# How q and k travel through DRAM in a multi-level attention kernel: long row runs against equal blocks of 16 rows

## The reference

```python
for lvl in range(4):
    x = query[:, ::2 ** lvl, :]
    q, k, v = split(x @ w_in[lvl].T + b_in[lvl])         # 16 heads of 16
    attn = softmax(q @ k.T / sqrt(16))
    outs.append((attn @ v) @ w_out[lvl].T + b_out[lvl])
current = outs[3]
for lvl in (2, 1, 0):
    current = upsample(current) @ up_w[lvl].T + up_b[lvl] + outs[lvl]
x = layernorm(x + current)
h = silu(x @ w1.T * s1) * (x @ w2.T * s2)
h = gelu(gelu(h @ h1.T * g1) @ h2.T * g2)
y = layernorm(x + h @ w3.T * s3)
```

## Time and profile before

| | us |
|---|---|
| median of 3 runs | 4259.68 |
| lowest and highest run | 4255.66, 4264.0 |
| the profiled execution | 4264.0 |
| its span, first to last instruction | 4262.2 |
| one regular batch of attention, from 1101.23 to 1431.91 us | 330.7 |

### The profile page before, as it was taken

How to read it: one execution, slowest core, us unless ns; L and a number is a source line. 1 busy time by engine, 2 the same in 40 slices (tenths; PEclk the granted TensorE clock), 3 DMA queues, 4 the chain that set the end, 5 groups by cost and what they waited for, 6 DMA issues and landing times. The chain is left out here.

```text
span 4262.2 us, 69758 instructions
## 1 busy us (share of the span) xinstructions
PE 3845.1 (90%) x20881; PEld 2140.1 (50%) x20881; DVE 2564.2 (60%) x4681; ACT 2486.9 (58%) x3261; POOL 1210.9 (28%) x1144
## 2 busy tenths in 40 slices
PE   4599999999989999989999999819999999999998
PEld 2233434434334433433433333207887787877887
DVE  2377787787787787787787788553333333333333
ACT  1377767767767767767767767624444433444343
POOL 4234444444434434534434442210000000000000
PEclk8699999999999999999999999959999999999999
DMA  5434434434333434333433432160000000000000
GB/s 184 107 79 98 102 90 104 101 87 98 100 91 89 109 73 111 101 81 98 108 90 83 115 89 57 34 237 6 13 18 11 11 11 21 11 11 12 17 14 11
DMA packets 277100, 307.45 MB, mean 72 GB/s; under 512 B 68000, under 2 KB 228960, under 8 KB 276448
## 3 DMA queue, kind: packets, MB, share of 16 engines
q1 hardware_dynamic: 267456, 293.56, 27.1%
q10 hardware_dynamic: 9216, 8.39, 0.6%
HBM read 202.28 MB, written 96.47 MB: 70 GB/s over the span
## 5 line engine op out<-in xcount | busy, mean ns | idle before, releaser
L766 ACT ACTIVATE a_probs<-a_p_s 128x1024 f32<-128x1024 f32 x1360 | 1326.4, 1021 | 625.4 <-PE a_p_s L1008 617.5
L847 DVE TENSOR_REDUCE a_part_max<-a_p_m 128x1 f32<-128x512 f32 x2048 | 1335.8, 680 | 407.1 <-PE a_p_m L1023 403.0
L1023 PE MATMUL a_p_m<-a_k_st,a_q_st 96*128 96x512 bf16 (+2 forms) x2944 | 1008.6, 375 | 172.7 <-DVE a_part_max L847 74.1
L1403 PE MATMUL p_h<-f_h_hi,f_w_hi 128*128 128x512 f32 x2048 | 810.2, 396 | 41.0 <-issue 38.7
L1008 PE MATMUL a_p_s<-a_q_st,a_k_st 98*128 98x512 bf16 (+2 forms) x2944 | 823.0, 367 | 3.2 <-DMA a_q_st<-a_neg_bf 2.3
L1403 PE MATMUL p_h<-f_h_lo,f_w_hi 128*128 128x512 f32 x2048 | 807.0, 394 | 1.8 <-issue 1.8
L1023 PEld LDWEIGHTS a_p_m<-a_k_st,a_q_st 96*128 96x128 bf16 x2944 | 257.5, 97 | 1068.2 <-DVE a_part_max L847 681.1
L1040 PE MATMUL a_p_o<-a_probs,a_v_aug 128*17 128x512 f32 (+2 forms) x5888 | 727.4, 573 | 0.8 <-ACT a_probs L766 0.8
L1372 DVE TENSOR_TENSOR f_h_lo<-f_h_f,f_h_hi 128x512 fp32r<-128x512 f32 x256 | 177.3, 693 | 722.4 <-ACT f_h_hi L1285 722.4
L847 DVE TENSOR_REDUCE a_row_max<-a_p_m 128x1 f32<-128x512 f32 (+2 forms) x672 | 439.9, 680 | 183.8 <-PE a_p_m L1023 178.0
L1283 ACT ACTIVATE f_h_f<-p_h,f_sc 128x512 f32<-128x512 f32 x256 | 176.6, 690 | 584.8 <-PE p_h L1403 584.7
(11 more groups left out here) (116 smaller groups left out, 4550.6 us busy)
## 6 DMA issues: line engine op xcount, KB each, us to landing
qk_scratch<-a_qk_bf SPq DMA_DIRECT2D x288, 128.0 KB
a_w_lo<-wqkv_inner SPq DMA_DIRECT2D x32, 768.0 KB, 5.0
a_q_st<-qk_scratch SPq DMA_DIRECT2D x32, 384.0 KB, 5.3
a_k_st<-qk_scratch SPq DMA_DIRECT2D x32, 384.0 KB, 6.8
a_a_lo<-a_attn SPq DMA_DIRECT2D x384, 32.0 KB, 2.0
a_o_lo<-wo_inner SPq DMA_DIRECT2D x24, 512.0 KB, 3.8
a_q_st<-qk_scratch SPq DMA_DIRECT2D x88, 128.0 KB, 4.5
a_k_st<-qk_scratch SPq DMA_DIRECT2D x88, 128.0 KB, 4.4
```

The source lines that it names most:

```text
L766: act.activation(probs[:, s % 2, 2 * p:2 * p + 2, :], p_s[:, 2 * p:2 * p + 2, :], ACT.Exp, scale=HD ** -0.5).then_inc(exp_done.sem, 1)
L847: dve.reduce_max(out, src, AX.X).then_inc(max_read.sem, 1)
L1023: ins = pe.matmul(p_m[:, n % 2, r * size:(r + 1) * size], q_st[0:ROWS, spot(unit, unit.blk, j) + q * 128:spot(unit, unit.blk, j) + (q + 1) ...
L1403: ins = pe.matmul(out, a, c, start=first and n == 0, stop=last and n == len(terms) - 1)
```

## The change

The lists of the pieces are written out: block `r` of 16 rows holds piece `K_PIECES[r]` of k and `Q_PIECES[r]` of q. The same six pairs are formed, in another order of rows. A projection's three pieces are stored by one DMA of 128 rows in place of three. A stack is loaded by twelve DMAs of 16 rows in place of six of 48, 32 and 16. DRAM holds the pieces as (q or k, piece, feature, token). `q_st` and `k_st` are laid out by half, head and token, so that at level 0 a head's 1024 tokens go into two runs of 512. The helpers `spot` and `placed` are gone, and PE's operands are addressed directly. PE, DVE and POOL have the same instructions in the same order, and ACT the same work.

```diff
--- before.py
+++ after.py
@@ -24,9 +24,9 @@
-PIECES = 3
-RUNS_OF_ROWS = ((0, 3, 0, 0), (48, 2, 0, 1), (80, 1, 0, 2))
-ROWS = 16 * sum(count for _, count, _, _ in RUNS_OF_ROWS)
+K_PIECES = (0, 0, 0, 1, 1, 2)
+Q_PIECES = (0, 1, 2, 0, 1, 0)
+ROWS = 16 * len(K_PIECES)
...
-        k_st = sb("k_st", [128, HALVES * HG * W], BF16)
-        q_st = sb("q_st", [128, HALVES * HG * W], BF16)
+        k_st = sb("k_st", [128, HALVES, HG, W], BF16)
+        q_st = sb("q_st", [128, HALVES, HG, W], BF16)
...
@@ -525,10 +514,8 @@
                             for i, (_, t, m, blk) in enumerate(PROJ[n]):
-                                for i_piece in range(PIECES):
-                                    slot = i_piece if t else PIECES - 1 - i_piece
-                                    sp.dma_start(scr[lvl][t, m * 8:(m + 1) * 8, slot, :, blk * W:blk * W + size],
-                                                 qk_bf[:, n % 2, i_piece, i * size:(i + 1) * size]).then_inc(stored[n % 2].sem, 16)
+                                sp.dma_start(scr[lvl][t, :, m * 128:(m + 1) * 128, blk * W:blk * W + size].rearrange("i p t -> p i t"),
+                                             qk_bf[:, n % 2, :, i * size:(i + 1) * size]).then_inc(stored[n % 2].sem, 16)
@@ -541,17 +528,24 @@
-                            for low, count, k_slot, q_slot in RUNS_OF_ROWS:
-                                for t, st, slot in ((0, q_st, q_slot), (1, k_st, k_slot)):
-                                    src = scr[lvl][t, unit.head:unit.head + heads, slot:slot + count, :, :].rearrange("h i d t -> (i d) h t")
-                                    size = heads * tokens(lvl)
-                                    dst = st[low:low + 16 * count, unit.halves[0] * HG * W:unit.halves[0] * HG * W + size].rearrange("p (h t) -> p h t", h=heads)
+                            for r in range(len(K_PIECES)):
+                                for t, st, pieces in ((0, q_st, Q_PIECES), (1, k_st, K_PIECES)):
+                                    src = scr[lvl][t, pieces[r], unit.head * 16:(unit.head + heads) * 16, :]
+                                    dst = st[16 * r:16 * r + 16, unit.halves[0]:unit.halves[0] + len(unit.halves), :, :]
+                                    if lvl == 0:
+                                        src = src.rearrange("(h d) (b t) -> d b h t", d=16, b=2)
+                                    elif across(lvl) == 1:
+                                        src, dst = src.rearrange("(h d) t -> d h t", d=16), dst[:, 0, :, :]
+                                    else:
+                                        src = src.rearrange("(h d) t -> d h t", d=16)
+                                        dst = dst[:, 0, :, :].rearrange("p h (i t) -> p (h i) t", i=across(lvl))
                                     sp.dma_start(dst, src).then_inc(stacked[n].sem, 16)
...
-    scr = [nc.dram_tensor(f"qk_scratch{i}", (2, H, PIECES, HD, tokens(i)), BF16, kind="Internal").ap() for i in range(LEVELS)]
+    scr = [nc.dram_tensor(f"qk_scratch{i}", (2, 3, E, tokens(i)), BF16, kind="Internal").ap() for i in range(LEVELS)]
```

## The result

The kernel after is slower, as forecast, by a third to a half of what was forecast: median 4292.77 us of 5 runs (4281.64 to 4312.08) against 4259.68 of 5 runs of before, ratio 1.0082, interval 1.0052 to 1.0111. It was timed twice more, each time beside a group of the experiments: 1.0034 (1.0020 to 1.0047) and 1.0066 (1.0044 to 1.0087). So the change costs 20 to 33 us by the medians, not 62. The three profiled executions of after have spans 13 to 22 us longer than that of before (4262.2), which was itself a long one: its time, 4264.0, is the highest of those five runs.

The account below looks back on a forecast made before the run. TensorE, busy 90% of the span, was taken as the bound, with late transfers as the cost: 7 x (1.6 + 3.5 + 2.0) = 49.7 plus opening 12.2, 62 us, gave 4326, or 4322 against the median; range 4296 to 4350, full 4278 to 4372.

Parts of the forecast that it names:

- Stores: Projection stores, three DMAs made one: complete on SP about 1.2 us earlier, worth nothing in the batches.
- Loads: Load of units 7 and 8: 16-row DMAs at 109 GB/s drain 4.8 us longer, issue takes 2.8 longer.
- Place A: Unit 14's attention packing, queued behind the load of units 7 and 8, lands 4.8 us later; PE loses 1.6, seven times.
- Place B: x1 stores behind load of units 9 and 10 land late, then unit 7's negated maxima; PE stands 3.5 us, seven times.
- Clock: After the stand at Place B, PE's clock falls to 0.50, costing 2.0 us a batch, between 0 and 4.
- Opening: Before the batches: first scores 8.6 us later, plus 3.6 at a load waited for in full, together 12.2 us.
- Rival 2: Batches: only one place bites, or the clock doesn't fall; 3.5 us a batch, 4296 us in all; chance 0.16.
- Rivals 1 and 4: 1: loads overlap, batches unchanged, 4265 us, chance 0.10; 4: shorter opening store chain, loads at 215 GB/s, 4247, chance 0.05.
- rival 3: Batches and opening: nothing covered, both delays 7.6 us, clock falls at both places; 120 us more, 4380; chance 0.15.

Follow-up runs that it names:

- twelve loads of wide rows: The kernel before with each load cut in two by heads, twelve DMAs of 48, 32 and 16 rows a stack: 4268.3 us, ratio 1.0034.
- spread rows: The kernel after with each DMA's 16 rows six partitions apart: 4344.54 us, ratio 1.0186; at the finest level only, 4261.9 us, ratio 1.0012.
- 96 rows: The kernel before with six scratch slots, a stack as two 96-row DMAs, stores with twice the bytes: 4244.08 and 4247.67 us, ratios 0.9982 and 0.9978.
- the packing first: The kernel after with unit 14's attention packing issued ahead of the load of units 7 and 8: 4272.98 us, ratio 1.0038.

## Why the prediction was right in direction and two to three times too large

*Stores.* By the landings in the traces, a projection's stores are complete 2.7 us behind their first issue against 4.8 before (medians of the regular batches; the expectation above has 4.6): 2.1 sooner, forecast 1.2. The prediction gave the old store 8 engines and the new one 16. The traces don't count engines, but the semaphore of an old store rises in 9 steps and that of a new one in 16, which points the same way. It is worth nothing in the batches, as said, and 9 us in the opening, which I had at under 3.

*Loads.* That the 16-row loads drain slowly was right and is shown from both sides: 16-row loads with the old stores take 14.9 us, twelve loads of wide rows 11.6, spread rows and 96 rows undo it. The rule behind it was not quite right. "The rate goes with how many rows are written at once" doesn't fit its own rows, where 48 rows move less than 32, and spread rows move 152 to 205 GB/s with 16 rows at a time: it is which rows, too. The size was off because I took 109 GB/s for the whole load from a stretch at its end. In the middle such DMAs follow each other and reach 127, so 3.8 us were added and not 4.8. The issue of the load of units 7 and 8 went from 2.7 to 8.7 us (medians), 6.0 more where I had 2.8: a DMA of 16 rows with eight pieces takes 0.60 us to issue, not 0.46.

*Place A*, forecast 1.6 us, measured 0.7 to 0.9. With 3.8 in place of 4.8 my own subtraction would have given 0.6.

*Place B*, forecast 3.5, measured 0.9 to 1.1 (2.1 once): the term that failed. Two things made it smaller. The load of units 9 and 10 takes 14.7 us against 11.5 (medians), 3.2 more and not 4.8. And 0.8 us are made up at SP, where the 127-row copy that the maxima land behind is issued 2.9 us after the fetch begins in before (median; 2.6 to 3.1) and 2.1 in after: in the batch with 3.1 one issue ahead of it took 1.44 us in before and 0.48 in after. So the maxima come 2.4 us later; their spare time in before was 1.3 us (median, 1.0 to 2.2), as forecast, and 1.1 is left. The forecast's sentence that none of this chain waits for PE was also wrong, but it cost nothing: the load is issued some 10 us ahead of PE's first maximum of unit 8 in before, in after and with the packing first, so it moves with PE, and B comes on top of A just as forecast.

*Clock*, forecast 2.0 us a batch, 14 in all: not found. The stands were 1 us and not 3.5, and the time at clock 0.50 is no longer than before. That a longer stand brings it is shown by the spread rows, where PE waits 5.8 us a batch (two waits, up to 4.8) and the clock is at 0.50 behind them in every batch. But there is one profile of before, and these stretches vary by 27 us between executions of the same kernel (47.8 and 75.1 in the two profiles with 96 rows), so a few microseconds of it can't be excluded.

*Opening*, forecast 12.2. First scores +5.5, +5.3, +3.0 in place of +8.6: the issues were underpriced (with the old stores +14.6, forecast 11.2 without the stores' gain) and the store's gain more so. The later wait for the load of units 7 and 8 was right:

```profile
212.68 0.61 PE L1017 MATMUL a_p_m<-a_k_st,a_q_st 96*128 96x512 bf16 x1 [11.63 <-DMA a_k_st<-qk_scratch]
```

11.63 against 8.14 is 3.5, forecast 3.6; but PE came 2.2 us sooner to that wait, so that only 1.3 us of the opening are left there (5.0 in the third profile).

Sum as measured: 7 x (0.8 + 1.0) is 12.6, the opening 1.3 to 5, together 14 to 18 us. With what each profile itself shows, the table's delay at the second batch and seven times its A and B, the sums are 20, 13 and 25 us for spans that are 20, 13 and 22 longer: little lies elsewhere in the profiles, and the part up to the second batch (7.2, 0.5, 4.9) differs between executions of one program, largely with the clock. The medians say 33, 20 and 26. In the first measurement the profiled execution of after was 9 us under its median and that of before 4 above, so 13 us of the 33 lie outside the two profiles and are not located. Rival 2 gave 4296, near the first measurement, but by another way: both places bite, each for a third of what one was to cost. Rivals 1 and 4 fell by the rate, rival 3 by its sizes.

## What to carry to other kernels

Cutting a load by rows cost twice here: DMAs that write 16 neighbouring rows drained more slowly (11.8 to 15.6 us a load), and more issues delayed what SP issues behind them (14 to 15 us in the opening with the old stores). Look for what is queued behind the transfer and count its spare time from landings: an extra delay of 3.8 us became stands of about 1. Check from issue times what moves along with the waiting engine before saying that a saving is given back. Here the best was to write all 96 rows at once (0.9978 and 0.9982). Rows far apart helped the large loads (1.0012), but everywhere they cost 80 us by their longer issue, so look at what stands behind them too.

## What was not expected of the hardware

Sixteen rows six partitions apart need about half of the DMA engines' time for more bytes per second than sixteen neighbours (share 0.53 to 0.66 at 152 to 205 GB/s, against 1.10 at 127). The issue of such a DMA on SP took 0.59 us where neighbouring rows of a coarse level took 0.43; at the finest level, with more pieces, both took 0.60. A store of x1 issued behind a copy of 127 rows landed after 5.6 to 6.9 us in the seven batches of after, and after 1.7 when the copy was cut into 112 and 15 rows. A stretch at clock 0.50 can be a good part of what two executions of one kernel differ by: 47.8 and 75.1 us in the same six batches.
